# Loading x and u of a matmul kernel in two transfers, of 16 and of 112 partitions

## The reference

```python
keep = (u >= P_DROP).astype(x.dtype)
x_drop = x * keep / (1.0 - P_DROP)
y = x + jnp.matmul(adj, x_drop)
out = (y - mean(y)) / sqrt(var(y) + 1e-5)      # over the last axis
```

## Time and profile before

| what | value |
|---|---|
| median of 3 runs | 642.15 us |
| profiled execution | 642.16 us |
| its span in the trace | 640.2 us |
| mean granted TensorE clock | 0.906 of full |
| read from memory | 272.63 MB |
| written to memory | 2.10 MB |

### The profile page before, as it was taken

The page is one execution under the profiler, slowest core; times in us unless marked ns, Lnnn a source line. Parts: engine busy times, 40 slices in busy tenths (PEclk is TensorE's granted clock), DMA queues, the critical chain, the costliest instruction groups (busy, mean ns, idle before and its releaser), DMA issues.

```text
span 640.2 us, 7695 instructions
## 1 busy us (share of the span) xinstructions
PE 510.8 (80%) x3458; PEld 263.7 (41%) x3458; DVE 60.8 (9%) x268; ACT 17.0 (3%) x24; POOL 1.1 (0%) x8
## 2 busy tenths in 40 slices
PE   0088798798788787887788878878977977979997
PEld 0044444444443443443444434433433443445435
DVE  1200100100100100010100110010010020020202
ACT  0000000000000000000000000000000000000000
POOL 0000000000000000000000000000000000000000
PEclk9997988988988987989978978978977987979999
DMA  9999999999999999999999999999999999999998
GB/s 385 430 431 447 427 430 450 430 430 447 434 430 424 445 434 404 430 434 439 430 434 447 430 430 450 430 430 440 436 434 399 458 438 407 435 424 431 434 419 354
DMA packets 7348, 274.80 MB, mean 429 GB/s; under 512 B 944, under 2 KB 1072, under 8 KB 1456
## 3 DMA queue, kind: packets, MB, share of 16 engines
q1 hardware_dynamic: 7200, 274.70, 99.5%
q10 hardware_dynamic: 144, 0.03, 0.0%
HBM read 272.63 MB, written 2.10 MB: 429 GB/s over the span
## 4 chain that ended last, share of the span: by engine, by line
DMA 66%; PE 33%; issue 0%; SPq 0%; DVE 0%; ACT 0%; ACTq 0%; DVEq 0%
DMA adj_ring<-adj_blocks 66%; PE acc L234 31%; PE tail_acc L234 2%; PE back L241 0%; SPq L151 0%; PE final L273 0%; SPq L153 0%; DVE x_and_u L342 0%; SPq L172 0%; ACT std L224 0%; DVE acc_sb L280 0%; ACTq L202 0%; DVE stats L336 0%; DVE mean_var L338 0%; DVE rstd L340 0%
## 5 line engine op out<-in xcount | busy, mean ns | idle before, releaser
L234 PE MATMUL acc<-adj_ring,x_and_u 128*64 128x320 f32 x3072 | 463.9, 467 | 99.4 <-ACTq L202 99.4
L234 PEld LDWEIGHTS acc<-adj_ring,x_and_u 128*64 128x64 f32 x3072 | 232.1, 148 | 326.2 <-ACTq L202 107.3
L280 DVE COPY acc_sb<-acc 128x320 f32<-128x320 f32 x24 | 10.7, 486 | 477.0 <-PE acc L234 477.0
L234 PE MATMUL tail_acc<-adj_ring,x_and_u 128*64 128x384 f32 (+1 forms) x256 | 29.1, 382 | 0.9 <-DMA adj_ring<-adj_blocks 0.8
L241 PE MATMUL back<-twofold,acc_sb 128*128 128x64 f32 x126 | 16.8, 280 | 11.9 <-DVE acc_sb L280 11.9
L196 ACT ACT_TABLE_LOAD x10 | 12.8, 1283 | 502.5 <-DMA adj_ring<-adj_blocks 502.5
L241 PEld LDWEIGHTS back<-twofold,acc_sb 128*128 128x128 f32 x126 | 15.0, 191 | 18.8 <-DVE acc_sb L280 18.7
L234 PEld LDWEIGHTS tail_acc<-adj_ring,x_and_u 128*64 128x64 f32 x256 | 15.7, 137 | 13.9 <-issue 9.8
L311 DVE TENSOR_SCALAR x_and_u<-summed,mean,rstd 128x64 f32 (+1 forms) x63 | 15.2, 310 | 0.5
L248 PE MATMUL final<-x_and_u,identity 128*128 128x64 f32 x2 | 0.7, 434 | 13.2 <-DMA x_and_u<-xu 13.2
L289 DVE BATCH_NORM_STATS2 stats<-summed 128x6 f32<-128x64 f32 x63 | 9.3, 213 | 0.4
(11 more groups left out here) (17 smaller groups left out, 7.4 us busy)
## 6 DMA issues: line engine op xcount, KB each, us to landing
adj_ring<-adj_blocks SPq DMA_DIRECT2D x23, 7680.0 KB, 33.3
adj_ring<-adj_blocks SPq DMA_DIRECT2D x11, 5120.0 KB, 36.8
adj_ring<-adj_blocks SPq DMA_DIRECT2D x1, 5760.0 KB, 28.0
adj_ring<-adj_blocks SPq DMA_DIRECT2D x1, 4480.0 KB, 30.0
x_and_u<-xu SPq DMA_DIRECT2D x1, 4096.0 KB, 12.4
adj_ring<-adj_blocks SPq DMA_DIRECT2D x1, 3840.0 KB, 23.3
adj_ring<-adj_blocks SPq DMA_DIRECT2D x1, 3072.0 KB, 30.3
adj_ring<-adj_blocks SPq DMA_DIRECT2D x1, 2560.0 KB, 35.7
```

The lines of the kernel that those rows point to most:

```text
L234: return nc.tensor.matmul(into[h * D:(h + 1) * D, 0:cols], x_drop[:, t * D:(t + 1) * D], adj_ring[:, at:at + cols], start=(t < 2), stop=(t ...
L280: last = nc.vector.tensor_copy(acc_sb[:, b * cols:(b + 1) * cols], part[:, 0:cols])
```

## The change

x and u come in two transfers in place of one: first partitions 0 to 15, one for each of the sixteen DMA engines, then partitions 16 to 127. Both add 16 to the same semaphore `x_loaded`, so the two engines that wait for it, PE and DVE, now wait for 32. Nothing else is changed.

```diff
+HEAD = 16
...
-            sp.dma_start(x_and_u[:], xu).then_inc(x_loaded, 16)
+            for part in (slice(0, HEAD), slice(HEAD, P)):
+                sp.dma_start(x_and_u[part, :], xu[part, :]).then_inc(x_loaded, 16)
             for s in range(SLOTS):
                 load(s, 0)
...
-            pe.wait_ge(x_loaded, 16)
+            pe.wait_ge(x_loaded, 2 * 16)
...
-            dve.wait_ge(x_loaded, 16)
+            dve.wait_ge(x_loaded, 2 * 16)
```

## The result

The kernel with two transfers takes 650.68 us (median, 650.57 to 650.78) beside 642.05 us for the kernel before in the same session: ratio 1.0134, 95% interval 1.0121 to 1.0146. It is slower by 8.6 us. The forecast of 647.0 us had the sign right and the place, the start of the stream, but only about half of the size, and the result lies 0.2 us above the stated range.

The account below looks back on a forecast made before the run. The prediction took an unbroken 432 GB/s load stream as the bound, so start losses are paid in full. First piece +4.25 and second +0.6 gave +4.85 on 642.15, forecast 647.0 us; stated range 641.3 to 650.5 us.

Parts of the forecast that it names:

- the stated range: Whole kernel: 641.3 to 650.5 us, meant to hold 8 in 10.
- What bounds the kernel: Whole span: a start, one unbroken load stream at 432 GB/s, and a tail; stream time lost at the start is paid in full.
- The issue and the waits: Start: one more SP issue (0.39 us, covered) and PE's and DVE's waits on 32 in place of 16; cost 0.
- The first piece: Start, transfer to partitions 0 to 15: +4.25 us, taking 5.46 us as the middle between 1.21 and 9.71.
- The high end: First piece: rate goes with the partitions addressed, 16 of 128 giving 54 GB/s and 9.71 us, cost +8.5 us.
- the low end: First piece: each engine carries one row at 27.0 GB/s, 1.21 us, cost 0, with a possible gain of 1.0 us.
- The second piece: Start, transfer to partitions 16 to 127: +0.6 us, the middle between 0 and +1.21 from scaling by 112 of 128.
- The forecast's own range: Whole kernel: 644.5 us (half of the middle) to 651.9 us (both high ends, +9.7).
- A: Rival on the x and u transfers: shape does not matter, engines carry rows at 27.0 GB/s; price 0, 642.15 us; chance 0.21.
- B's head start: Rival, first 3 us: one row per engine gives the last engine work early; at most -1.0 us, 641.4 us; chance 0.15.
- C's gap: Rival, between the two pieces: engines finish before the second transfer comes, 1.7 us once, 643.9 us; chance 0.06.
- The signs: Start: x and u land at 16 to 20 us, windows from 2 to 7 us about 100 GB/s, first product at 35 to 37.

Follow-up runs that it names:

- e8: Kernel before, with all 128 partitions of x and u loaded once more ahead of everything, as a control: 651.78 us beside 642.06.
- e1: Changed kernel, but both transfers of 128 partitions, first the x half, then the u half, same waits on 32: 642.08 us beside 642.06.
- e6: Kernel before, with partitions 0 to 15 loaded once more ahead of everything, x and u then whole: 646.03 us beside 642.06.
- p1: Kernel before plus thirteen separate loads ahead; (3) 16 rows to every eighth partition 4.7 us, (5) 64 rows to 0-63 12.5, (6) to 32-95 7.4.
- p2: Kernel before plus eight four-load bursts; 2: partitions 0-15, 111 GB/s; 4, 5: every 7th from 16, from 0, later rows 2.36-2.45, 2.5-2.6 us.
- e7: Kernel before, with partitions 16 to 127 loaded once more ahead of everything, x and u then whole: 656.34 us beside 642.06.
- e3: Changed kernel with HEAD = 64 in place of 16, so partitions 0 to 63, then 64 to 127: 652.62 us, ratio 1.0165.
- e2: Changed kernel, but the first 512 KB as 128 partitions x 4,096 bytes, then the other 28,672 bytes of each partition: 642.12 us, ratio 1.0.
- e4: Changed kernel with its pieces in the other order, partitions 16 to 127 first, then 0 to 15: 652.37 us, ratio 1.0159.
- p3: Kernel before plus eight four-load bursts, every 4th partition; 2 from 36: pair's rows 2.41-2.42 us; 3 from 40: 208 GB/s; 4 from 48: rows 2.56 us.

## Where the prediction was right, and the step that failed

*What bounds the kernel: right.* An unbroken stream in which every microsecond lost at the start is paid at the end. e8 adds 9.72 us for 9.71 us of bytes, and the stretch from 40.45 to 640.85 us has the same 1.00 and 432 GB/s as the earlier trace rows.

*The issue and the waits: right.* e1 has both and costs 0.0 us. In the changed kernel x_drop has 10.6 us to spare where the prediction had 10.7.

*The first piece: right in kind, too large.* Its term was +4.25 us, the middle between no loss and a rate that goes with the number of partitions. e6 has +2.8. The high end rested on a rate by partition count, and p1 (3), (5) and (6) show that it isn't the count. Sixteen neighbours get a quarter of the rate and not an eighth (111 GB/s, p2 burst 2), and their first rows are through sooner still (3.6 us in the change, 4.8 later in a burst). The reason given for not taking the low end was a loose reading: between the first and the last slice has rates from 399 to 458 GB/s, not one number. The estimate from the Trainium skill's page "SBUF — State Buffer", section on door 1, gave +3.8 for this piece, nearer to the measured 2.8 than the middle of the two ends, and the 111 GB/s agree with its rule of four ports.

*The second piece: this step failed.* Its term was +0.6 us, and e7 has +5.8. These 5.2 us are more than the 3.7 that the whole forecast missed, since the first piece's term was too large.
*The range.* The forecast's own range, to 651.9 us, held the result, but by luck: its top, +9.7, is 8.5 for the first piece and 1.2 for the second, and the runs have 2.8 and 5.8. The stated one ended at 650.5, 0.2 us short. It was cut there by a chance of 0.07 for the top, which was too small for a case whose second term had only been scaled.

*The rivals.* A is refuted by e1 against e3: two transfers and the same bytes in both, +0.0 and +10.6 us. B's head start doesn't show in the time of e2. C's gap is not there: in the change's packets the large piece's rows start where the first rows end.

*The signs.* Those named for a right forecast came in the right direction, but more strongly: x and u were to land at 16 to 20 us and landed at 22.3, the first product was to start at 35 to 37 us and started at 40.5. The windows from 2 to 7 us were to show about 100 GB/s and the later ones 432; they show 176, then 274 and 218, and these two belong to the second piece. The place named as most likely to be wrong was the first piece's middle; it was off by 1.5 us, the second piece's term by 5.2.

Left open: why two pairs hold up all and one pair doesn't; how 112 rows are dealt to sixteen engines; why the other order costs 1.7 us more (e4); and the 0.7 us given back between the first and the second wait of PE. No version tried beats the kernel before: e1 and e2 equal it.

## What to carry to other kernels

Cut a large transfer by columns, not by partitions: the same 512 KB ahead cost nothing as 128 x 4 KB (e2) and 2.8 us beyond their bytes as 16 x 32 KB (e6). Sixteen rows for sixteen engines isn't sixteen lanes; ask where the rows land, and ask it of the remainder too, since the piece with 112 of 128 partitions lost twice as much as the piece with 16. And read GB/s beside the DMA share: a share of 1.00 stood over 432 GB/s and one of 0.99 over 214 (p3, burst 4).

## What the runs showed of the hardware that was not expected

Two pairs of engines, by the map each pair on one path, bring all sixteen to 2.4 to 2.6 us for a row of 32,768 bytes (p2, bursts 4 and 5; p3, burst 3), where one pair leaves the other fourteen at the 1.21 us of a lone engine (p3, burst 2). A busy share is time occupied, and an engine that is held up counts as busy (0.97 at 208 GB/s, p3, burst 3). And 64 partitions can be as fast as they need be or half as fast by their position alone: 7.4 us at 32 to 95, 12.5 us at 0 to 63 (p1, 6 and 5).
